# Attention, gate and feed-forward kernel: which engine does the large element-wise work of the prologue, and in what order the first head's keys and bias tables are fetched

## What is computed

```
x = x + attention(layernorm(x));  x = x + ffn(layernorm(x))          x: [4, 1024, 128] f32
attention: k, v, q = split(x @ w_in);  16 heads of width 8
  bias[h, r]  = sum over 21 k of amplitudes[h,k] * exp(-|sharpness[h,k]| * (r - offsets[h,k])^2),  r = -1023..1023
  weights     = softmax(q @ k^T / sqrt(8) + bias[h, key - query])
  out         = weights @ v;   a, g = split(out @ w_gate + b_gate);   returns a * sigmoid(g)
ffn: FP8-quantised x and weight, matrix product, bias, rounded to bf16
```

## Time and profile before

| | before |
|---|---|
| runs, median (lowest to highest) | 625.1 us (624.92 to 625.32), 3 runs |
| profiled execution, own time | 626.02 us |
| its span, first to last instruction | 624.2 us |
| PE, DVE, ACT, POOL busy share | 93%, 91%, 88%, 16% |
| first scores of the head loop (L935) | 68.31 us |
| last work of the head loop on PE (L960) starts | 560.80 us |

### The profile page before, as it was taken

One profiled execution on the slowest core, in us unless ns is written; L12 is line 12 of the kernel. 1 busy time (PEld: TensorE's weight loads), 2 busy tenths in 40 slices (PEclk: granted clock), 3 DMA queues, 4 the chain that ended last, 5 costly groups with the idle time before them and its releaser, 6 DMA issues.

```text
span 624.2 us, 12750 instructions
## 1 busy us (share of the span) xinstructions
PE 579.9 (93%) x4026; PEld 158.0 (25%) x4026; DVE 565.8 (91%) x689; ACT 551.2 (88%) x614; POOL 101.1 (16%) x94
## 2 busy tenths in 40 slices
PE   7977499999999999999999999999999999999945
PEld 3534012222222222222222222222222222224522
DVE  8995589999999999999999999999999999974885
ACT  3555489999999999999999999999999999993475
POOL 6661400010101010101010101100010101011640
PEclk9789599999999999999999999999999999999968
DMA  7144710504141414232332323132414141410004
GB/s 177 68 119 120 234 44 3 147 20 148 25 140 33 132 52 117 70 94 82 90 91 74 102 63 107 58 114 51 117 48 123 44 127 40 126 25 9 1 0 135
DMA packets 29483, 52.63 MB, mean 84 GB/s; under 512 B 9437, under 2 KB 20698, under 8 KB 28506
## 3 DMA queue, kind: packets, MB, share of 16 engines
q1 hardware_dynamic: 27560, 51.83, 29.7%
q10 hardware_dynamic: 1906, 0.60, 0.4%
HBM read 42.35 MB, written 9.16 MB: 83 GB/s over the span
## 4 chain that ended last, share of the span: by engine, by line
ACT 41%; issue 36%; PE 9%; DVE 8%; DMA 2%; SPq 1%; ACTq 1%; POOL 1%; DVEq 0%
ACT pbuf L1037 17%; ACT split L1037 17%; DVE pbuf L484 3%; ACT pbuf L1045 3%; PE ps L1239 3%; ACT split L1045 2%; PE ps L1283 1%; DMA t64s<-gl_scratch 1%; SPq L303 1%; PE ps L960 1%; PE ps L1234 1%; PE ps L935 1%; DMA x_sb<-in_L_attn_x 1%; ACT o_sbs L787 1%; ACTq L1036 1%
## 5 line engine op out<-in xcount | busy, mean ns | idle before, releaser
L994 DVE TENSOR_TENSOR split<-ps,t 128x1024 f32<-128x1024 f32 x192 | 231.9, 1223 | 14.4 <-PE ps L935 9.1
L994 DVE TENSOR_TENSOR pbuf<-ps,t 128x1024 f32<-128x1024 f32 x192 | 230.2, 1217 | 14.9 <-PE ps L935 10.9
L1037 ACT ACTIVATE pbuf<-pbuf 128x1024 f32<-128x1024 f32 x192 | 208.0, 1272 | 11.3 <-DVE pbuf L994 11.1
L1037 ACT ACTIVATE split<-split 128x1024 f32<-128x1024 f32 x192 | 203.4, 1281 | 1.9 <-DVE split L994 1.9
L935 PE MATMUL ps<-qb,kb 33*128 33x512 f16 x1024 | 184.4, 391 | 16.8 <-DMA t64s<-gl_scratch 9.8
L960 PE MATMUL ps<-pbuf,vst 128*32 128x512 f32 x1024 | 137.8, 610 | 0.0
L960 PE MATMUL ps<-split,vst 128*32 128x512 f32 x1024 | 136.0, 604 | 1.0 <-ACT split L1045 1.0
L935 PEld LDWEIGHTS ps<-qb,kb 33*128 33x128 f16 x1024 | 48.6, 93 | 304.4 <-DVE pbuf L994 113.9
L944 PE MATMUL ps<-t64s,ident 128*64 128x512 f16 x512 | 80.5, 395 | 0.0
L1045 ACT ACTIVATE split<-ps 128x1024 f32<-128x1024 f32 x64 | 79.4, 1240 | 0.0
L1045 ACT ACTIVATE pbuf<-ps 128x1024 f32<-128x1024 f32 x64 | 79.0, 1235 | 0.0
(11 more groups left out here) (151 smaller groups left out, 335.9 us busy)
## 6 DMA issues: line engine op xcount, KB each, us to landing
t<-g_scratch SPq DMA_DIRECT2D x16, 960.0 KB
kb<-k_scratch SPq DMA_DIRECT2D x120, 64.0 KB
t64s<-gh_scratch SPq DMA_DIRECT2D x16, 248.0 KB
t64s<-gl_scratch SPq DMA_DIRECT2D x16, 248.0 KB
qb<-q_scratch SPq DMA_DIRECT2D x60, 64.0 KB
x_sb<-in_L_attn_x SPq DMA_DIRECT2D x4, 512.0 KB, 7.7
q_scratch<-split SPq DMA_DIRECT2D x8, 256.0 KB, 2.7
k_scratch<-split SPq DMA_DIRECT2D x8, 256.0 KB, 2.8
```

Of the source, the lines that this page charges most:

```text
L994: eng.tensor_tensor(slot(g, b), banks(unit(k), 2), t128[p][:, t * P:t * P + S], ALU.add).then_inc(z_ready, 1)
L1037: eng.activation(buf, buf, ACT.Exp).then_inc(p_ready, 1)
```

## The change

- POOL no longer computes `gauss[2]`; ACT squares all three groups, directly from `off` (scale -1, so that it squares offset - r), with a semaphore `off_in` of its own, so it need not wait for the other parameters; `noff` and its DVE instruction are gone.
- POOL's `square` instructions, six instead of seven, come only after the last normalisation (`xn_ready`, 4) and after `sel_ready`. The square of batch 2's keys goes to ACT.
- POOL fills the first head's `vst` (two memsets) at the start in place of DVE.
- DVE: `normalise(2)` ahead of `moments(3)`; the scaling of `sel` and the cast to `hselb` after `normalise(3)`; batch 1's value copy comes from ACT to DVE; the five instructions on `bg_parts` go to the end of the head loop.
- ACT: `k_high(2)` ahead of `turn(3)`.
- SP: keys in a part of three batches (`MOST`) and a part of one (`LAST`); the bias table loads ahead of the last four key copies; the `bg_parts` store and its reading back go behind the loop, ahead of the last loads of the head outputs.
- PE: 40 instead of 44 matmuls on zeros.

```diff
--- before.py
+++ after.py
@@ -51,7 +51,7 @@
-WARM_START = 44
+WARM_START = 40
 WARM_TURN = 5
@@ -295,12 +295,12 @@
-        def load_keys(eng, part, rows, half):
-            t = slice(half * 2 * S, (half + 1) * 2 * S)
+        def load_keys(eng, part, rows, t):
             for c in range(2):
...
                     eng.dma_start(kb[0][ROW * c + r:ROW * c + r + HD, t], split[0:HD, part, t]).then_inc(first_in, 16)
+        MOST, LAST = slice(0, (B - 1) * S), cols(B - 1)
@@ -323,24 +323,22 @@
                 store_qk(eng, 0, qk_out)
-                eng.wait_ge(kh_ready, 2)
-                load_keys(eng, 2, (0, 8), 0)
                 store_qk(eng, 1, qk_out)
-                load_keys(eng, 3, (16, 24), 0)
+                eng.wait_ge(kh_ready, B - 1)
+                load_keys(eng, 2, (0, 8), MOST)
                 store_qk(eng, 2, qk_out)
+                load_keys(eng, 3, (16, 24), MOST)
                 eng.wait_ge(gh_ready, 2)
...
                 eng.wait_ge(kh_ready, B)
-                load_keys(eng, 2, (0, 8), 1)
-                eng.wait_ge(kl_ready, B)
-                load_keys(eng, 3, (16, 24), 1)
+                load_keys(eng, 2, (0, 8), LAST)
                 eng.wait_ge(g_out, 16 * 3)
...
                 load_bias_parts(eng, 0, 0, head_in[0])
-                eng.wait_ge(bg_ready, 1)
-                eng.dma_start(bg_dram.rearrange("(o a) c -> o a c", o=1), bg_parts[:, :, :]).then_inc(bg_out, 16)
+                eng.wait_ge(kl_ready, B)
+                load_keys(eng, 3, (16, 24), LAST)
                 eng.wait_ge(consts_in, 64)
@@ -357,6 +355,10 @@
                 eng.memset(pick[:, :, :], 0.0).then_inc(pick_ready, 1)
+                for n, (dst, value) in enumerate(value_fills(0)):
+                    if n:
+                        eng.wait_ge(values_filled, 1)
+                    eng.memset(dst, value).then_inc(values_filled, 1)
@@ -381,32 +383,29 @@
                 inverse_std(0)
-                eng.wait_ge(par_ready, 1)
-                eng.tensor_scalar(gauss[2], rel, off[:, 2:3], None, ALU.subtract).then_inc(shifted_ready, 1)
-                inverse_std(1)
-                eng.wait_ge(shifted_ready, 1)
-                eng.tensor_tensor(gauss[2], gauss[2], gauss[2], ALU.mult).then_inc(shifted_ready, 1)
-                inverse_std(2)
-                square(0, 0, qh_ready)
-                inverse_std(3)
                 eng.wait_ge(pick_ready, 1)
...
                         eng.tensor_copy(pick[:, i, r + HD * i:r + HD * i + HD], ident[:, 0:HD]).then_inc(pick_ready, 1)
+                for b in range(1, B):
+                    inverse_std(b)
+                eng.wait_ge(xn_ready, B)
+                eng.wait_ge(sel_ready, 1)
+                square(0, 0, qh_ready)
                 square(0, 1, kh_ready)
...
                 square(2, 0, qh_ready)
-                square(2, 1, kh_ready)
                 square(3, 0, qh_ready)
...
                 with nc.allow_non_contiguous_dma(reason="336 parameters"):
-                    for dst, name in ((off, "offsets"), (shp, "sharpness"), (amp, "amplitudes")):
+                    for dst, name, done in ((off, "offsets", off_in), (shp, "sharpness", par_in),
+                                            (amp, "amplitudes", par_in)):
                         eng.dma_start(dst[:, :], io[name].rearrange("h k -> (h k)")
-                                      .rearrange("(g p) -> p g", p=PP)).then_inc(par_in, 16)
+                                      .rearrange("(g p) -> p g", p=PP)).then_inc(done, 16)
                 eng.dma_start(ident[:, :], io["c_ident"]).then_inc(ident_in, 16)
@@ -416,14 +415,14 @@
                         eng.wait_ge(rel_in, 1)
+                        eng.wait_ge(off_in, 16)
+                    eng.activation(gauss[g], rel, ACT.Square, bias=off[:, g:g + 1], scale=-1.0)\
+                       .then_inc(square_ready, 1)
+                def gaussian(g):
+                    if g == 0:
                         eng.wait_ge(par_ready, 1)
-                    eng.activation(gauss[g], rel, ACT.Square, bias=noff[:, g:g + 1]).then_inc(square_ready, 1)
-                def gaussian(g):
-                    if g < 2:
-                        eng.wait_ge(square_ready, g + 1)
-                    else:
-                        eng.wait_ge(shifted_ready, 2)
+                    eng.wait_ge(square_ready, g + 1)
                     eng.activation(gauss[g], gauss[g], ACT.Exp, scale=nshp[:, g:g + 1]).then_inc(exp_ready, 1)
@@ -457,11 +456,12 @@
-                for step, n in ((square, 0), (square, 1), (turn, 0), (gaussian, 0), (q_high, 0), (k_high, 0),
-                                (turn, 1), (gaussian, 1), (q_high, 1), (v_copy, 0), (k_high, 1), (turn, 2),
-                                (gaussian, 2), (q_high, 2), (v_copy, 1), (turn, 3), (k_high, 2), (bias_copies, 0),
-                                (q_high, 3), (k_high, 3), (k_square, 3), (v_copy, 2), (first_queries, 0),
-                                (first_queries, 1), (v_copy, 3), (first_queries, 2), (first_queries, 3)):
+                for step, n in ((square, 0), (square, 1), (square, 2), (turn, 0), (gaussian, 0), (q_high, 0),
+                                (k_high, 0), (turn, 1), (gaussian, 1), (q_high, 1), (v_copy, 0), (k_high, 1),
+                                (turn, 2), (gaussian, 2), (q_high, 2), (k_high, 2), (turn, 3), (k_square, 2),
+                                (bias_copies, 0), (q_high, 3), (k_high, 3), (k_square, 3), (v_copy, 2),
+                                (first_queries, 0), (first_queries, 1), (v_copy, 3), (first_queries, 2),
+                                (first_queries, 3)):
                     step(n)
@@ -500,8 +500,7 @@
                 moments(0)
-                eng.wait_ge(par_in, 48)
-                eng.tensor_scalar(noff[:, :], off[:, :], -1.0, None, ALU.mult)
+                eng.wait_ge(par_in, 32)
                 chain(eng, eng.tensor_scalar(nshp[:, :], shp[:, :], -1.0, None, ALU.mult))
@@ -516,27 +515,19 @@
                 stats_of(3)
+                normalise(2)
                 moments(3)
-                normalise(2)
+                q_low(1)
+                k_low(1)
+                normalise(3)
                 eng.wait_ge(sel_in, 32)
...
                 last.then_inc(sel_ready, 1)
-                q_low(1)
-                k_low(1)
-                normalise(3)
                 q_low(2)
-                for n, (dst, value) in enumerate(value_fills(0)):
-                    if n:
-                        eng.wait_ge(kb_filled, 3)
-                    eng.memset(dst, value).then_inc(kb_filled, 1)
-                eng.wait_ge(bgate_in, 16)
-                chain(eng, eng.tensor_copy(bg_parts[:, 0, :], bgate[:, :]))
-                chain(eng, eng.tensor_tensor(bgate[:, :], bgate[:, :], bg_parts[:, 0, :], ALU.subtract))
-                chain(eng, eng.tensor_copy(bg_parts[:, 1, :], bgate[:, :]))
-                chain(eng, eng.tensor_tensor(bgate[:, :], bgate[:, :], bg_parts[:, 1, :], ALU.subtract))
-                eng.tensor_copy(bg_parts[:, 2, :], bgate[:, :]).then_inc(bg_ready, 1)
+                eng.wait_ge(v_ready, 2)
+                eng.tensor_copy(v_all[:, tiles(1), :].rearrange("p n d -> p (n d)"), banks(6, 2)).then_inc(v_copied, 1)
                 k_low(2)
@@ -669,10 +660,10 @@
                 eng.wait_ge(hsel_ready, 1)
-                eng.wait_ge(sq_ready, 2 * B - 1)
+                eng.wait_ge(sq_ready, 2 * B - 2)
                 norms(0)
                 eng.wait_ge(ql_ready, B)
-                eng.wait_ge(sqk_ready, 1)
+                eng.wait_ge(sqk_ready, 2)
                 norms(1)
@@ -852,8 +843,6 @@
                 store_qk(eng, B - 1, qk_out)
-                eng.wait_ge(bg_out, 16)
-                eng.dma_start(bg_rows[:, :], bg_dram).then_inc(bg_out, 16)
                 eng.wait_ge(filled, FIRST + LATER)
@@ -882,6 +871,10 @@
+                eng.wait_ge(bg_ready, 1)
+                eng.dma_start(bg_dram.rearrange("(o a) c -> o a c", o=1), bg_parts[:, :, :]).then_inc(bg_out, 16)
+                eng.wait_ge(bg_out, 16)
+                eng.dma_start(bg_rows[:, :], bg_dram).then_inc(bg_out, 16)
                 eng.wait_ge(o_stored[0], 16 * B * (NH2 + 1))
@@ -889,7 +882,8 @@
-                eng.wait_ge(kb_filled, 4)
+                eng.wait_ge(kb_filled, 2)
+                eng.wait_ge(values_filled, 2)
                 copy_v(eng, 0, 0)
@@ -1022,6 +1016,12 @@
                             eng.reciprocal(dc[0][:, :], dc[0][:, :]).then_inc(inv_ready[0], 1)
+                eng.wait_ge(bgate_in, 16)
+                chain(eng, eng.tensor_copy(bg_parts[:, 0, :], bgate[:, :]))
+                chain(eng, eng.tensor_tensor(bgate[:, :], bgate[:, :], bg_parts[:, 0, :], ALU.subtract))
+                chain(eng, eng.tensor_copy(bg_parts[:, 1, :], bgate[:, :]))
+                chain(eng, eng.tensor_tensor(bgate[:, :], bgate[:, :], bg_parts[:, 1, :], ALU.subtract))
```

(3 more changed lines are left out.)

2 lines of the change are left out of this document (removed).

## The result

The changed kernel takes 615.98 us (median; 615.85 to 617.81) against 625.21 us for the kernel before, measured beside it: a ratio of 0.9847, 95% interval 0.983 to 0.9864, so 9.2 us less. The prediction was 614.3 with a range of 610.5 to 618. The profiled execution took 615.97 us with a span of 614.1; before these were 626.0 and 624.2. In one execution against one execution the gain is therefore 10.1 us, and in the medians 9.2. Executions of one kernel differ with the mean granted clock of TensorE: three of the four of the changed kernel took 615.85 to 615.99 us at 0.971, the fourth 617.81 at 0.963.

The account below looks back on a forecast made before the run. Bound: the prologue's chain of waits over DVE's normalisations, SP's issue queue and the bias tables' landing. First scores at 57.5 instead of 68.3, 10.8 less, give 626.0 to 615.2; the median, 0.9 lower, gives 614.3; range 610.5 to 618.

Parts of the forecast that it names:

- `normalise` at 2.5 us: DVE in the prologue: batches 0, 1 and 3 fall from 7.1, 5.4 and 6.6 us to batch 2's 2.5.
- ACT's third square and DVE's memset at nothing: Prologue: the square's 1.95 is covered before transposed x arrives; the memset does not wait for POOL, 1.0 kept for the range.
- Stores issued at 40.5: SP's queue: the bias vectors' stores start 8.2 behind the release at 32.3, at 40.5 instead of 49.38.
- Stores land after 9.1: SP's wait before the tables: the three bias vectors' stores land 9.1 behind first issue, so SP waits until 49.6.
- Tables in 7.9: Bias table loads take 7.9 from the wait's end to landing at 57.5, bounds 6.7 and 8.7; last keys land about then.
- Batch 3's stores covered: Head loop's start: batch 3's stores land by 63.5, DVE's third group wants them at 66; covered by 2.7.
- The first groups' pace unchanged: Head loop's first groups: PE stands still ahead of the loop as before, some 9 us, so their pace stays.
- The end at nothing: Loop's end: five `bg_parts` instructions, 2.1, lie in DVE's wait of 3.47; priced at nothing, 2 in reserve.
- A: Rival, 13%: the bias vectors' stores do not hold SP, landing within 5 us; first scores 15 earlier, 610.
- B: Rival, 17%: prologue moves less (held memset, casts, slower key issue, later key landing); 2 to 4 less gain, 617.5.
- C: Rival, 3%: POOL did not cause the slow `normalise`, batches 0 and 1 stay slow; 2 less, 623.
- D: Rival, 2%, the only slower case: SP stands at `bg_ready` at the end, giving the gain back and more; over 625.

Follow-up runs that it names:

- experiment 1: The changed kernel with the third group of squares (`gauss[2]`) back on POOL, beside `normalise(0)` and `normalise(1)`: 624.81 us, ratio 0.9994 to the kernel before.
- experiment 4: The kernel before with SP's part alone (keys of three batches and one, the last ones behind the tables): 629.88 us, ratio 1.0076.
- experiment 5: The changed kernel with SP's order of key copies and tables as before the change, the `bg_parts` store still behind the loop: 613.52 us.
- experiment 7: The changed kernel with the three stores of the bias vectors ahead of the second four key copies: 614.41 us.
- experiment 6: The changed kernel with the last four key copies ahead of SP's wait for the bias vectors' stores: 616.8 us.
- experiment 2: The changed kernel with one more POOL instruction, a fill of an unused 128x2048 tile beside `normalise(0)`: 618.2 us, one execution.
- experiment 3: The kernel before with POOL's part alone; DVE's order and fills, SP's order and the small `bg_parts` instructions as before: 620.83 us, ratio 0.9911.
- experiment 8: The changed kernel with the bias vectors' stores ahead of the second four key copies and all keys ahead of the wait: 616.33 us.
- experiment 9: The changed kernel with 58 matmuls of zeros in TensorE's wait for the tables: 616.94 us.
- experiment 10: The changed kernel with SP's old order of key copies and tables, and 38 matmuls of zeros in TensorE's wait: 612.42 us.

## Why the prediction was right, and where its terms were off

Mechanism, sign and range held; the gain was 0.7 short on the profile's own time (10.8 predicted, 10.1 found), and the time 1.7 above the forecast (615.98 against 614.3). The other 0.9 is the allowance for the profiled execution before being above its median: the one after was at its median. Two of the prediction's own marks of failure were met. The tables were issued after 51, and the loop changed by over 1 (492.5 to 491.3 us from first scores to last products). The two errors ran against each other: the first scores came 2.3 later than predicted, and the loop with 1.2 and the end with 0.3 gave most of it back. That these 1.5 us, priced at nothing, made up for the mis-sized wait was luck.

- *`normalise` at 2.5 us*: measured 2.12 to 2.14. The group of batch 2, from which the 2.5 was taken, was not the floor. The 0.3 for POOL's casts was not there either (they stand at 9.85 to 10.44 beside `normalise(0)`, which took 2.14). `k_low(1)` ended at 26.70 instead of 27.7.
- *ACT's third square and DVE's memset at nothing*: right. ScalarE did the square from 9.36 to 11.35 and transposed x arrived at 13.31; the memset still started at 3.47.
- *`k_high(2)` ends at 32.3*: measured 31.43.
- *Stores issued at 40.5*: measured 40.83. The 0.9 won so far was lost in SP's queue: twelve issues took 9.4 us, not 8.2; the four stores alone took 3.3 instead of 2.6. **Issue times of before were a lower bound for a queue that now runs fuller.**
- *Stores land after 9.1*: the mis-sized term that counts. Here 11.3 (40.83 to 52.15), in experiment 1 11.6 and in experiment 4 11.2. The wait and its place were as predicted. The 9.1 was right for the order of before and wrong for the new one, and the prediction's own reading of packets of 1 KB (those under 2 KB less those under 512 B) shows it. From 46.5 on the changed kernel has 256 of them, as many as the two 16-bit vectors have rows of 512. The last of them fall in 51.5 to 52 in the changed kernel, at most 11.2 behind the first issue, and in 45 to 45.5 with SP's part undone, at most 8.6 behind it (36.95). The first line is the changed kernel at 51.5 to 52, the others are experiment 5 at 45 to 45.5 and 45.5 to 46:

```profile
DMA packets 12, 0.01 MB, mean 25 GB/s; under 512 B 3, under 2 KB 9, under 8 KB 12
```

```profile
DMA packets 50, 0.07 MB, mean 146 GB/s; under 512 B 12, under 2 KB 39, under 8 KB 50
...
DMA packets 23, 0.05 MB, mean 98 GB/s; under 512 B 11, under 2 KB 11, under 8 KB 23
```

  With the stores ahead of the second four key copies (experiment 7) the last ones fall in 47.5 to 48, at most 10.1 behind the first issue. Each of these ends is known to 0.5. So the new order of key copies made the stores some 2.6 longer, and the four just ahead of them account for some 1.1 of it. A part lies in the issue: the three stores took SP 3.4 us (40.83 to 44.24), with SP's part undone 1.8. The Trainium skill, DMA: Bandwidth & Descriptors, section Why a DMA increments its semaphore by 16 and not by 1, ties a transfer's share of the 16 engines to the outer dimension of its access patterns. The estimate made from this and the page's cost of a transfer, 6.8 us, was further off than the packets. No run split the stores over more engines.
- *Tables in 7.9*: from 52.15 to the first scores 7.6. Tables and last keys arrive close together, as predicted (experiment 6).
- *First scores at 57.5*: 59.76, from + 0.3 at the issue, + 2.2 at the landing, - 0.3 at the tables.
- *Batch 3's stores covered*: right. The first add that writes over `split` starts 8.0 us behind the first add, as before, and VectorE is idle for 0.50 ahead of it, before 0.49.
- *The first groups' pace unchanged*: off by 0.9 in these two executions, and for a reason that did not hold: TensorE stood still ahead of the loop for 13.3 us, not some 9 as before. The clock came back sooner after the start than before. On the kernel before the stretch 78 to 82, 9.7 us behind the first scores, has a mean clock of 0.71; on the changed one the stretch 68 to 72, 8.2 behind them, has 0.80. Experiment 6, with the same start, has 0.61 in 70 to 72, where the changed kernel has 1.00, and is 0.9 later at the thirteenth add. So the 0.9 is not shown to be the change's.
- *The end at nothing*: right; 1.75 us of the cover are left, and the end is 0.3 shorter. That the five instructions took at most 0.41 before was a misreading: the fifth took 1.87, beside a POOL square. At the loop's end they take 0.27 to 0.41.
- *Rivals*: A fell with the 11.3. B's doubts came true in part (issues 1.2 longer); the larger miss, the stores' landing, was in none of the rivals. C fell with experiments 1 and 2; D did not occur.

What the prediction did not ask is whether each part of the change helps. By experiments 3, 4 and 5, POOL's part alone gives 4.4 us, SP's part alone costs 4.7, both are worth 9.2 with the small instructions moved, and all but SP's part gives 12.4. SP's part takes away 2.5 by the medians: it waits for a third batch of keys ahead of everything and removes the cover over the stores. The small instructions moved away from POOL's squares, priced at nothing, are by an estimate most of the difference between 4.4 and 12.4: four of them by 1.5 us are 6. The other moves of VectorE and ScalarE (fills, value copy, `k_high(2)` ahead of `turn(3)`) are in this difference too. None of these moves was run by itself.

The Trainium skill, SBUF — State Buffer, section Who interferes with whom, was borne out three times: 5487, 1796 and about 1900 ns on VectorE beside 5.45, 1.80 and about 1.9 us on POOL.

## What to carry to other kernels

When one instruction of a group has a maximum as long as another engine's instruction, look at which instructions of both meet, and ask of a moved instruction what stands beside its new place: small ones can pay its full length. A wait for a landing that other issues cover costs nothing until the order is changed; price it from a kernel with the same queue ahead of it, and try the change without the reordering. Measure a start not by the first instruction but by the first one at the steady pace, since the clock can give back or take away microseconds between the two; and compare several executions, since one kernel's differ by 2 us with its mean granted clock.

## What was not expected of the hardware

- The VectorE instructions with an operand in PSUM were not held by POOL. Beside the same squares (29.50 to 40.65), those of the changed kernel, two of them shown, keep their length, while the casts and subtractions of experiment 3 on SBUF alone took 1.9 to 2.0. A fill of 128x1024 on VectorE was not held either: 0.91 us beside the squares of experiment 3 (at 33.06), 0.91 with POOL idle in the kernel before (at 43.20). The squares and the two instructions of the changed kernel:

```profile
29.50 11.15 POOL L375 TENSOR_TENSOR pbuf<-split 128x1024 bf16<-128x1024 f16 x6 [2.87 <-DVE pbuf L484]
```

```profile
29.75 1.23 DVE L491 TENSOR_TENSOR split<-ps,split 128x1024 f16<-128x1024 f32 x1 [0.38 <-ACT split L434]
30.89 1.22 DVE L530 COPY v_all<-ps 128x1024 f32<-128x1024 f32 x1
```

- The issue of one transfer on SP takes 0.54 to 0.7 us, but up to 2.79 in experiment 7 and 3.08 in experiment 8, with no wait in the program just before it.
- Three stores of bias vectors take up to 8.6 us to land in one order of the queue and 11.2 in another, though a store of 256 KB lands in 2.6.
- Between the last zero matmul and the first scores pass 1.25 us on TensorE in both experiments 9 and 10. It is SP that releases them, and the meeting of the engines ahead of the loop lies in this time.
